# Rows of one partition laid end to end: token 4p+t instead of token 128t+p on partition p of tile t

## Time and profile before

| | us |
|---|---|
| median of 3 runs | 1187.3 |
| lowest, highest | 1186.52, 1191.24 |
| profiled execution, own time | 1182.42 |
| its span | 1180.7 |
| TensorE matmul busy | 1019.0 (86% of the span) |
| VectorE, ScalarE, GpSimd busy | 830.3, 742.6, 632.6 |
| DMA: moved, mean rate | 107.47 MB, 91 GB/s |

### The profile page before, as it was taken

The page is one execution under the profiler, slowest core; times in us unless marked ns, Lnnn a source line. Parts: engine busy times, 40 slices in busy tenths (PEclk is TensorE's granted clock), DMA queues, the critical chain, the costliest instruction groups (busy, mean ns, idle before and its releaser), DMA issues. The chain is left out here.

```text
span 1180.7 us, 31510 instructions
## 1 busy us (share of the span) xinstructions
PE 1019.0 (86%) x8446; PEld 608.8 (52%) x8446; DVE 830.3 (70%) x2411; ACT 742.6 (63%) x1311; POOL 632.6 (54%) x1195
## 2 busy tenths in 40 slices
PE   4488888988888898987788998866999999999875
PEld 3453333333333333333345665535888888888732
DVE  5677887778777877777779998433666666666637
ACT  4577777777777767775655666414666666666616
POOL 4236666666666666664423777771444444444344
PEclk9899999999999999998996999878999999999988
DMA  8313333333332333333243111112222222221166
GB/s 217 94 47 93 99 96 103 95 100 87 97 108 86 99 95 99 100 99 111 71 150 115 54 54 57 54 60 68 61 64 64 64 58 63 62 65 54 43 224 210
DMA packets 135606, 107.47 MB, mean 91 GB/s; under 512 B 32203, under 2 KB 127874, under 8 KB 135538
## 3 DMA queue, kind: packets, MB, share of 16 engines
q1 hardware_dynamic: 124722, 87.45, 26.3%
q0 software_dynamic: 8544, 17.78, 4.2%
q10 hardware_dynamic: 2272, 1.45, 0.4%
HBM read 55.96 MB, written 50.69 MB: 90 GB/s over the span
## 5 line engine op out<-in xcount | busy, mean ns | idle before, releaser
L1542 DVE TENSOR_REDUCE maxima<-ps 128x8 f32<-128x1024 f32 x320 | 381.2, 1220 | 119.4 <-PE ps L1164 107.3
L916 ACT ACTIVATE pT_area<-ps 128x1024 f32<-128x1024 f32 x320 | 327.1, 1024 | 138.0 <-PE ps L1196 136.8
L704 POOL TENSOR_SCALAR_AFFINE_SELECT pT_area<-pT_area 128x256 f32<-128x256 f32 (+1 forms) x448 | 190.3, 439 | 103.7 <-ACT pT_area L916 103.2
L806 POOL DMA_INDIRECT ys_dram<-quad_area,place_cur x139 | 133.0, 957 | 192.6 <-issue 135.7
L1237 PE MATMUL ps<-pT_area,quad_area 128*32 128x512 f32 (+3 forms) x2048 | 190.7, 446 | 0.0
L796 POOL DMA_INDIRECT xs_dram<-quad_area,idx_cur x128 | 123.1, 962 | 74.9 <-issue 73.6
L1196 PE MATMUL ps<-quad_area 64*128 64x512 bf16 (+3 forms) x1024 | 125.5, 302 | 39.4 <-DVE maxima L1542 37.9
L1404 PE MATMUL ps<-quad_area 128*128 128x256 f32 (+1 forms) x456 | 130.0, 367 | 6.3 <-issue 4.5
L1405 PE MATMUL ps<-quad_area 128*128 128x256 f32 (+1 forms) x456 | 128.5, 364 | 0.0
L1164 PE MATMUL ps<-quad_area 61*128 61x128 bf16 (+2 forms) x1792 | 126.2, 242 | 0.0
L1024 ACT ACTIVATE xnT<-ps,be_cur 128x256 f32<-128x256 f32 (+1 forms) x228 | 94.4, 447 | 47.6 <-PE ps L1405 47.3
(11 more groups left out here) (237 smaller groups left out, 1523.1 us busy)
## 6 DMA issues: line engine op xcount, KB each, us to landing
qk_dram<-split_area SPq DMA_DIRECT2D x192, 128.0 KB, 2.3
quad_area<-qk_dram SPq DMA_DIRECT2D x256, 96.0 KB, 2.3
row_area<-xs_dram SPq DMA_DIRECT2D x63, 132.0 KB
pT_area<-ys_dram SPq DMA_DIRECT2D x16, 512.0 KB, 5.0
pT_area<-in_L_ffn_We SPq DMA_DIRECT2D x12, 384.0 KB, 7.0
out_dram<-pT_area SPq DMA_DIRECT2D x7, 512.0 KB, 2.9
xs_dram<-row_area SPq DMA_DIRECT2D x5, 528.0 KB, 4.2
split_area<-in_L_ffn_We SPq DMA_DIRECT2D x12, 192.0 KB, 3.6
```

The costliest lines, as they stand in the source:

```text
L704: return pool.affine_select(out=blocks, in_=blocks, compare_op=ALU.is_ge, fill=0.0, base=0, pattern=[[0, count], [1, P]], channel_multipli ...
L806: pool.indirect_dma_start(ys_dram, at, ys[:, ns % 2, h, :], None).then_inc(s_yst[ns % 2], 16)
L916: act.activation(pT[:, gs % 2, n, :], ps[:, bank:bank + 2, :].rearrange("p a b -> p (a b)"), ACT.Exp).then_inc(s_exp, 1)
L1542: dve.tensor_reduce(to, ps[:, bank:bank + 2, :].rearrange("p a (j k) -> p a j k", k=P), AX, ALU.max).then_inc(s_mxf, 1)
```

## The change

Partition p now holds tokens 4p to 4p+3 of a batch, token 4p+t in tile t. Loads of x move 2 KB per partition and batch in one run, stores of the result the same, and `ys_dram` is laid out by partition (row 128p + 2*(4b+t) + k), so that a pick moves 4 KB per partition in one run. Since the attention needs tokens in order, the four transposes of `turn_xn` now each write every fourth column of the PSUM bank, and `project_y` reads every fourth column of `yT` as its stationary operand. Nothing else of the instruction streams changes: the same number of DMAs, matmuls and waits.

```diff
+        ys_rows = ys_dram[0:2 * TILES * P].rearrange("(p t k) c -> p t k c", t=TILES, k=2)
...
+        def every_fourth(columns, t):
+            return columns.rearrange("p (r t) -> p t r", t=NT)[:, t, :]
...
         def load_x(engine, n):
             first, last = X_LOADS[n]
-            engine.dma_start(x_sb[:, NT * first:NT * last, :],
-                             a["L0_attn_x"][first:last].rearrange("b (t p) c -> p (b t) c", p=P)).then_inc(s_x[n], 16)
+            engine.dma_start(x_sb[:, NT * first:NT * last, :].rearrange("p (b t) c -> p b (t c)", t=NT),
+                             a["L0_attn_x"][first:last].rearrange("b (p t) c -> p b (t c)", t=NT)).then_inc(s_x[n], 16)
...
             def pick(n):
                 for h in range(2):
-                    at = 2 * (R * n + NT * h) * P
-                    sp.dma_start(picked[:, n % 3, NT * h:NT * h + NT].rearrange("p t k c -> p t (k c)"),
-                                 ys_dram[at:at + 2 * NT * P].rearrange("(t p k) c -> p t (k c)", p=P, k=2)).then_inc(s_pick[n % 3], 16)
+                    at = R * n + NT * h
+                    sp.dma_start(picked[:, n % 3, NT * h:NT * h + NT].rearrange("p t k c -> p (t k c)"),
+                                 ys_rows[:, at:at + NT].rearrange("p t k c -> p (t k c)")).then_inc(s_pick[n % 3], 16)
...
-                        sp.dma_start(out[2 * n - 4 + h].rearrange("(t p) c -> p t c", p=P),
-                                     final[:, n % 2, NT * h:NT * h + NT]).then_inc(s_out[n % 2], 16)
+                        sp.dma_start(out[2 * n - 4 + h].rearrange("(p t) c -> p (t c)", t=NT),
+                                     final[:, n % 2, NT * h:NT * h + NT].rearrange("p t c -> p (t c)")).then_inc(s_out[n % 2], 16)
...
-                    sp.dma_start(out[2 * n - 4:2 * n - 2].rearrange("b (t p) c -> p (b t) c", p=P), final[:, n % 2]).then_inc(s_out[n % 2], 16)
+                    sp.dma_start(out[2 * n - 4:2 * n - 2].rearrange("b (p t) c -> p b (t c)", t=NT),
+                                 final[:, n % 2].rearrange("p (b t) c -> p b (t c)", t=NT)).then_inc(s_out[n % 2], 16)
...
-            pool.iota(tag_i[:, BLANKS:BLANKS + 2 * TILES], pattern=[[1, 2], [2 * P, TILES]], base=0, channel_multiplier=2)
+            pool.iota(tag_i[:, BLANKS:BLANKS + 2 * TILES], pattern=[[1, 2], [2, TILES]], base=0, channel_multiplier=2 * TILES)
...
-                    last = pe.transpose(ps[:, xT_bank(b), t * P:(t + 1) * P], xn[:, b % 2, t, :], ident[:])
+                    last = pe.transpose(every_fourth(ps[:, xT_bank(b), :], t), xn[:, b % 2, t, :], ident[:])
...
-                    last = pe.matmul(ps[:, bank, t * C:(t + 1) * C], yT[:, ns % 2, t * P:(t + 1) * P], w_proj[:],
+                    last = pe.matmul(ps[:, bank, t * C:(t + 1) * C], every_fourth(yT[:, ns % 2, :], t), w_proj[:],
```

## The result

| | before | after |
|---|---|---|
| median of 20 runs each, us | 1185.66 | 1188.51 |
| lowest, highest, us | 1181.08, 1191.24 | 1185.38, 1192.52 |
| profiled execution, own time, us | 1182.42 | 1187.12 |

The ratio is 1.0024, 95% interval 1.0013 to 1.0035: 2.9 us slower, where 0.6 us faster was forecast. The interval is 1.5 to 4.1 us, inside the half per cent that the prediction called no change, but it excludes both 1 and the forecast's direction.

The account below looks back on a forecast made before the run. It took GpSimd's constants to bound the prologue, GpSimd's scatters the shared part, TensorE the experts and the final stage's pairs. Gains of 0.2 (picks) and 0.4 (stores) made 0.6 us, 1187.3 to 1186.7; range 1182 to 1196.

Parts of the forecast that it names:

- part 5: Strided weight loads in `project_y`: 0 taken; high end +0.92 us a batch, 1.8 to 6.4 before the first scatter.
- Part 4: The 64 transposes writing every fourth column: 0 taken, from float32's 0.83 ns a column; high end 5.1 us.
- Part 1: Loads of x in the prologue, 2 KB runs: 0 taken, as GpSimd's constants end last; ends -0.5 and 0.
- Part 2: First picks of the final stage, 4 KB runs for 1 KB: 0.2 us gained; ends 1.0 gained, 0.9 lost.
- Part 3: Result stores at the end, 2 KB runs for 512 B: 0.4 us gained for both together; ends 0 and 0.6.
- Part 6: Expert results scattered to other rows: 0 taken, 2.6 us to spare; wrong if the median landing leaves 2.2 us.
- A: Rival, chance 0.12: strided TensorE operands cost time, doubling transposes and weight loads, 6.9 us; 1193.6, at most 1198.2.
- B: Rival, chance 0.13: DMA pieces don't matter, a fixed cost of issue and receipt governs the transfers; 1187.3 us.
- C: Rival, chance 0.04: 64 KB distances in DRAM slow landings from 2.2 to 3.2 us, and the picks by 0.9; 1192.6.
- D: Rival, chance 0.05: ScalarE's single 5.2 us wait for something the profile calls remote may go; 1181.5 us.

Follow-up runs that it names:

- e4: The changed kernel with plain transposes and plain `project_y` reads, leaving only longer DMA runs and new row numbers: 1185.69 us, ratio 1.0000 to the kernel before.
- e5: The changed kernel with the strided `project_y` read only in the first seven batches, plain in the other nine: 1187.43 us, ratio 1.0014 to the kernel before.
- e6: The changed kernel with the strided `project_y` read only in the last nine batches: 1184.91 us, ratio 0.9997 to the kernel before.
- e3: The kernel before with only the transposes of `turn_xn` writing every fourth PSUM column: 1186.31 us, ratio 1.0003.
- e7: The changed kernel with `project_y` reading columns 1, 2, 3, 4 apart (loads 189, 197, 261, 329 ns) and a strided bfloat16 bias write (597 ns instead of 384).
- e2: The kernel before with only `project_y` reading every fourth column of `yT` as stationary operand: 1191.65 us, ratio 1.0051.
- e11: The changed kernel with the strided `project_y` read only in the first four batches: 1186.79 us, ratio 1.0013 to the kernel before.
- e10: The kernel before with only the strided `project_y` read, the same edit as e2 run again: 1190.17 us, ratio 1.0037.
- e8: The changed kernel with the transposes of `turn_y` writing the sorted order and `project_y` reading plain columns: 1186.73 us, ratio 1.0009 to the kernel before.

## Why the prediction was wrong

The forecast's direction failed by one term, part 5.

*Part 5, `project_y`: the step that failed.* The prediction took 0, "as both weight loads of a matmul run beside the matmul before". They do run beside it, but that hides a load only while loads can start as close together as the matmuls do. Plain, each matmul and its load came 0.11 us after the ones before at the full clock; strided, a load needs 0.23, and the matmuls then come at the load's pace, since nothing else of them was changed. Its high end, +0.92 a batch, was the true size (0.97). It also counted well what such a size would cost: between 1.8 (by VectorE's two waits in the earlier trace rows) and 6.4 (seven batches on the path). The path took 3.4 in the profiled execution and 2.7 in the pair of e4 and e5. VectorE's waits in the same view of the kernel after:

```profile
DVE st L1755 <- PE ps L1306: 9.1, 3, 6.7
```

That is 2.6 us more than the 6.5 of before, in three waits for two: another engine's waits in the trace before were too low a price, because the added time makes TensorE last where it was not. And seven batches at the full price were too many: three of them run at half the clock, where plain loads come 0.21 us apart as well. Four batches at 0.97 are 3.9, the last three take 0.15 to 0.31 each, together 0.6; that 1.1 of these 4.5 us falls into slack is inferred, no run shows where. That the later nine would cost "0 or so" held (e6).

*Part 4, transposes:* 0, right (four in 0.60 us, e3). The argument from density, 0.83 ns a column, says that a strided bfloat16 write has no such room, and e7 agrees in direction. That density is why the float32 transposes are free is argued, not shown.

*Part 1, loads of x:* 0 on the path, right, with 12.52 for the power. The load itself was taken too fast: about 400 GB/s came only between 12 and 14 us, the mean was 350, and x landed by 16 us, not 13.

*Part 2, first picks:* 0.2 taken, 0.0 measured. Runs of 1 KB were long enough already: 383 GB/s with either, and e2 has 4.85 us with 1 KB. Its end of 1.0 gained doesn't quite add up either, 0.2 and a third of 2.15 being 0.9. *Part 3, stores:* 0.4 taken, 0.2 + 0.2 measured.

*Part 6, scattered rows:* 0, right. The median landing went from 2.2 to 2.3 us, and leaving 2.2 was the sign set for part 6 being wrong; but VectorE waited less on these scatters (27.8 us in 53 waits, 29.8 in 56 before), and the experts' stretch is as long with either layout (328.2 and 328.3 us in the mean):

```profile
DMA to landing us min/median/max: 2.2/2.3/4.2
```

*The rivals.* A, "strided TensorE operands cost time", was given 0.12 and was half true: its mechanism holds for the weights alone, and 6.9 us was too much since the doubled transposes (5.1 of it) aren't there. B, "the pieces don't matter", is true of the picks only. C is out: with distances of 64 KB a landing takes 2.3 us, not 3.2, and the first pick 4.79 to 4.95. D, the hole: the wait of ScalarE fell from 5.2 to 4.0 us, and e4 has no gain from it.

```profile
ACT v_all L850 <- remote: 4.0, 1, 4.0
```

The sum by what the runs show: -0.4 (stores) + 2.7 to 3.4 (early projections) = +2.3 to +3.0 us, measured +2.9 (1.5 to 4.1). The starting point was off as well: the median of three runs, 1187.3, is 1.6 us over that of twenty, 1185.66.

*What stays open.* e5 strides in all seven early batches, has 47.70 us, and should by this sum be 3.8 slower, but measured 1.7 (0.1 to 3.2). e11 should be 3.0 and measured 1.5 (0.2 to 3.0). Single ratios carry some 1.5 us of doubt either way, and which granted clock an execution takes in this stretch was read only for the profiled ones: against plain traces of its own clock e5 should be 2.3 slower. Why the strided weights alone (e2, e10) lose more than the whole change isn't explained beyond the lower granted clock of their stretch and the stores' 0.4.

## What to carry to other kernels

A strided stationary operand isn't free because the load overlaps: compare how close together the loads can start with how close together the matmuls start, since the slower of the two sets the pace. The lengths of their records overlap and don't tell it. Bound such an unknown by the number of instructions before the next engine's work starts, not by who waited in the trace before, and leave out those behind a full queue of another engine. If an order must change between two layouts, let the operation that isn't at its limit do it: here a float32 transpose into PSUM or a ScalarE copy out of it sorted for nothing.

## What the runs showed of the hardware

- The record of a load of 128 float32 columns as the stationary operand lasted 189, 197, 261 and 329 ns for columns 1, 2, 3 and 4 apart. In `project_y` such loads start 0.11 us apart plain and 0.23 four apart. The slow load keeps its time when the granted clock halves: eight take 1.94 us at either clock, where the plain eight rise from 0.97 to 1.78.
- A 512-column bfloat16 matmul writing every fourth float32 column of PSUM took 597 ns for 384. A 128-column float32 transpose took 273 ns with neighbouring columns, 273 with a step of 4 columns (e3) and 273 with jumps of 512 bytes (e8). A median can lie higher with or without a step: 282 in the kernel after and 291 in e10, where they are plain, with a granted clock of 0.89 over the first 75 us in both (0.91 in e3).
- Loads in runs of 512 B moved 289 GB/s, in runs of 2 KB 350 in the mean of 12 us and 403 in the best 2. Between runs of 1 KB and 4 KB there was no difference (383). Stores in runs of 2 KB landed 0.2 us sooner than in runs of 512 B, in each trace that had them.
